# The opening of a retrieval-and-scoring kernel: products nobody reads ahead of the user's part, the second list's products behind chunk 0, chunk 1's load behind slot 6, tile 2's sort behind chunk 0's low part

## What is computed

```
retrieved = jnp.mean(item_embeddings[indices], axis=1)          # indices 512 x 50, table 12500 x 512
fused_rep = jnp.concatenate([user_rep, retrieved], axis=1) @ W_fuse + b_fuse   # 512 x 1024 @ 1024 x 512
logits    = fused_rep @ W_proj + b_proj                          # 512 x 512 @ 512 x 12500, fp32
```

## Time and profile before

| | us |
|---|---|
| median of 3 runs | 310.73 (309.54 to 311.03) |
| the profiled execution | 309.87 |
| its span | 308.0 |
| TensorE busy in it | 296.9 (96%) |
| VectorE busy | 248.3 (81%) |
| ScalarE busy | 128.1 (42%) |
| GpSimd busy | 74.9 (24%) |
| granted TensorE clock, mean | 1.000 |

### The profile page before, as it was taken

One profiled execution on the slowest core, in us unless ns is written; L12 is line 12 of the kernel. 1 busy time (PEld: TensorE's weight loads), 2 busy tenths in 40 slices (PEclk: granted clock), 3 DMA queues, 4 the chain that ended last, 5 costly groups with the idle time before them and its releaser, 6 DMA issues.

```text
span 308.0 us, 4024 instructions
## 1 busy us (share of the span) xinstructions
PE 296.9 (96%) x1384; PEld 242.3 (79%) x1384; DVE 248.3 (81%) x371; ACT 128.1 (42%) x164; POOL 74.9 (24%) x76
## 2 busy tenths in 40 slices
PE   3999999699999999999999999999999999999995
PEld 1559887498888889888887888888888888888884
DVE  5898998778987836999689989979799797996123
ACT  1104664430010012435375575655846458463310
POOL 4766886787777200000000000000000000000000
PEclk9999999999999999999999999999999999999999
DMA  7999999999996322367538966839677494343315
GB/s 271 337 377 312 358 400 377 409 361 403 291 304 211 107 100 69 130 226 277 198 137 324 318 257 220 313 136 292 240 239 295 146 360 159 135 138 128 131 70 199
DMA packets 32547, 75.13 MB, mean 244 GB/s; under 512 B 4511, under 2 KB 20655, under 8 KB 32528
## 3 DMA queue, kind: packets, MB, share of 16 engines
q1 hardware_dynamic: 25264, 58.06, 52.6%
q0 software_dynamic: 5536, 13.73, 13.6%
q10 hardware_dynamic: 1728, 3.10, 2.6%
HBM read 52.85 MB, written 25.60 MB: 255 GB/s over the span
## 4 chain that ended last, share of the span: by engine, by line
PE 80%; DMA 10%; DVE 6%; issue 1%; ACT 1%; POOL 0%; SPq 0%; POOLq 0%; DVEq 0%; ACTq 0%
PE pair L1137 25%; PE pair L1215 15%; PE pair L1217 15%; PE pair L1218 15%; DMA early<-w_proj 7%; PE pair L1083 4%; PE pair L1123 3%; DMA ring<-item_embeddings,rows 2%; DVE w_lo L833 2%; DVE w_lo L919 1%; DMA early<-w_fuse 1%; DVE pair L796 1%; PE pair L1168 0%; DVE t_sums L908 0%; PE pair L1089 0%
## 5 line engine op out<-in xcount | busy, mean ns | idle before, releaser
L440 POOL DMA_INDIRECT ring<-item_embeddings,rows x56 | 59.8, 1067 | 20.3 <-issue 14.0
L1137 PE MATMUL pair<-w_hi,f_hi 128*128 128x500 f32 x144 | 56.7, 394 | 1.8 <-DVE w_lo L833 1.8
L1137 PE MATMUL pair<-w_lo,f_hi 128*128 128x500 f32 x144 | 56.3, 391 | 0.0
L1137 PE MATMUL pair<-w_hi,f_lo 128*128 128x500 f32 x144 | 56.0, 389 | 0.0
L1215 PE MATMUL pair<-w_hi,s_hi 128*128 128x500 f32 x128 | 49.9, 390 | 0.0
L1217 PE MATMUL pair<-w_lo,s_hi 128*128 128x500 f32 x128 | 49.9, 390 | 0.0
L1218 PE MATMUL pair<-w_hi,s_lo 128*128 128x500 f32 x128 | 49.8, 389 | 0.0
L796 DVE SCALAR_TENSOR_TENSOR pair<-ring,mask,pair 128x512 f32<-128x512 f32 x48 | 36.1, 752 | 3.3 <-DVE pair L810 0.5
L1215 PE MATMUL pair<-w_hi,f_hi 128*128 128x500 f32 x96 | 37.3, 389 | 0.1
L1218 PE MATMUL pair<-w_hi,f_lo 128*128 128x500 f32 x96 | 37.2, 388 | 0.0
L1217 PE MATMUL pair<-w_lo,f_hi 128*128 128x500 f32 x96 | 37.2, 387 | 0.0
(11 more groups left out here) (138 smaller groups left out, 433.2 us busy)
## 6 DMA issues: line engine op xcount, KB each, us to landing
w_raw<-w_proj SPq DMA_DIRECT2D x26, 500.0 KB, 8.1
early<-w_proj SPq DMA_DIRECT2D x24, 500.0 KB, 6.7
logits<-part_out SPq DMA_DIRECT2D x21, 500.0 KB, 3.4
logits<-out_sb SPq DMA_DIRECT2D x28, 250.0 KB, 2.3
logits<-out_sb SPq DMA_DIRECT2D x10, 500.0 KB, 3.0
logits<-out_sb ACTq DMA_DIRECT2D x8, 250.0 KB, 7.0
early<-b_proj SPq DMA_DIRECT2D x8, 250.0 KB, 9.9
s_sum<-b_proj SPq DMA_DIRECT2D x8, 250.0 KB, 6.9
```

Source lines behind the costliest of these rows:

```text
L440: return nc.gpsimd.indirect_dma_start(out=to, out_offset=None, in_=table, in_offset=bass.IndirectOffsetOnAxis(ap=column, axis=0), **how)
L1137: m = nc.tensor.matmul(ps[:, 0:CHUNK], f[:, t, k, :], w, start=begin, stop=(f is f_lo and k == HK - 1))
```

## The change

Six edits, all in the first 65 us of the program:

- TensorE starts with 16 products of 256 columns into `total_ps`, which nothing reads; their operand is a piece of the still unused `w_hi`, which VectorE sets to 1.0 as its first instruction (`warm_ready`).
- The products of list 1 (`pack_list(1)`) move from behind the user's part to behind chunk 0 of tile 0. `list_spots(1)` moves behind `split_lo(0)` and has its own scratch in `out_sb`; `list_rows(1)` and `list_taken(1)` move behind `split_lo(2)`. List 1 has a PSUM bank of its own, so that group 2 waits for `list_kept`, the first evacuation waits for both lists, and group 0 and ScalarE's first split wait for list 0 alone.
- `list_rows(0)` and `list_taken(0)` stand behind slot 5's add, not slot 3's. `bias_lo` moves behind `add_last(0)`.
- SyncE loads `wf_ret` ahead of chunk 1, and waits for slot 6 of tile 0 ahead of chunk 1.
- `sort(2)` moves from ahead of `count_columns` to behind `list_spots(1)`. `split_lo(1)` is cut in two around the first f_lo, `split_lo(5)` around `add_home(1)`.
- In chunk 7 of tile 0 `turn_slots` stands directly ahead of `turn_sum(1)`, and both stand ahead of the wait for the second half's low part.

```diff
             sp.dma_start(bf_col[:], b_fuse).then_inc(bf_landed, 16)
+            sp.dma_start(wf_ret[:], wf_dram[1]).then_inc(wf_ret_landed, 16)
+            sp.wait_ge(slot_landed[place(0, 6)], 16 * slot_uses(0, 6))
             load_chunk(1)
-            sp.dma_start(wf_ret[:], wf_dram[1]).then_inc(wf_ret_landed, 16)
...
                 act.wait_ge(projected, c + 1)
+                if c == 0:
+                    act.wait_ge(packed, LISTING)
...
-            act.wait_ge(packed, LISTING)
+            act.wait_ge(packed, 1)
             split_hi(0)
             split_hi(1)
             mean(0)
...
+            nc.vector.memset(warm[:, 0:2 * P].bitcast(F32), 1.0).then_inc(warm_ready, 1)
             number()
...
             sort(1)
-            sort(2)
             count_columns()
             list_spots(0)
-            for i in range(4):
+            for i in range(DVE_FIRST - 1):
                 add(0, i)
             list_rows(0)
             list_taken(0)
-            list_spots(1)
-            for i in range(4, DVE_FIRST):
-                add(0, i)
-            bias_lo()
+            add(0, DVE_FIRST - 1)
             count_left()
             add_last(0)
+            bias_lo()
             dve.wait_ge(laps_ready, 2)
             add_home(0)
             split_lo(0)
-            list_rows(1)
-            split_lo(1)
+            list_spots(1)
+            sort(2)
+            split_lo(1, (0,))
             fused_lo(0, (0,))
+            split_lo(1, (1,))
             add_last(1)
             fused_lo(0, (1,))
             add(1, 0)
             fused_lo(0, (2, 3))
             add(1, 1)
+            split_lo(2)
+            list_rows(1)
             list_taken(1)
-            split_lo(2)
...
-            split_lo(5)
+            split_lo(5, (0,))
             add_home(1)
+            split_lo(5, (1,))
...
             def turn_sum(t):
                 if t == 1:
+                    turn_slots()
...
                 for k in range(HK):
+                    if halfway is not None and k == HK // 2:
+                        turn_sum(halfway)
                     if (begun or c == RESIDENT and t == 0) and k % 2 == 0:
                         pe.wait_ge(lo_ready, 2 * c + k // 2 + 1)
                     if first:
                         pe.wait_ge(f_ready, HK * t + k + 1)
-                    if halfway is not None and k == HK // 2:
-                        turn_sum(halfway)
...
                 if g == 0:
                     pe.wait_ge(bias_lo_ready, 1)
-                    pe.wait_ge(listed, LISTING)
+                    pe.wait_ge(listed, 1)
+                elif g == 1:
+                    pack_list(1)
+                elif g == 2:
+                    pe.wait_ge(list_kept, LISTING)
...
+            pe.wait_ge(warm_ready, 1)
+            for x in range(WARM):
+                nc.tensor.matmul(total_ps[:, 0:2 * P], warm[:, 0:P], warm[:, 0:2 * P], start=True, stop=True)
             user_part(0)
...
             user_part(3).then_inc(user_fused, 1)
-            pack_list(1)
```

21 lines of the change are left out of this document (12 added, 9 removed).

## The result

| | before | after |
|---|---|---|
| median, us | 310.6 (309.54 to 311.46, 12 runs) | 311.43 (310.9 to 312.97, 12 runs) |
| ratio to before | | 1.0033 [1.0019, 1.0047] |
| the profiled execution, us | 309.87 | 311.04 |
| its span, us | 308.0 | 309.2 |
| home add of tile 0 starts, us | 27.63 | 24.92 |

The change made the kernel slower by a third of a per cent: a small loss, but the ratio's interval lies above 1, and the median lies above the predicted range. The granted clock is 1.000 in both. From the start of fuse(1) to the end of the execution it takes 311.04 - 64.81 = 246.2 us, before 309.87 - 63.96 = 245.9 us: of the 1.17 us between the two executions 0.85 are there when fuse(1) starts. The table shows the path: the home add is 2.7 us earlier, and ten microseconds behind it VectorE is late.

What follows compares the result with a forecast made beforehand. The start of fuse(1) was taken to bound the kernel, set by landings, VectorE's queue and TensorE's products. 0.45 us at chunk 6 and 0.1 at chunk 7 put it 0.5 us earlier: median 309.8 us, range 308.2 to 311.1.

Steps and rivals of the forecast that it cites:

- The moment that decides: Start of fuse(1) on TensorE, at 63.96 us before: the whole change is worth its shift; 244 us of products follow.
- Unread products at 0: TensorE's start: 16 products might save 2.0 us in the user's part, but nothing on the path, behind slot 10's landing.
- List 1's products covered: TensorE between chunks 0 and 1: 1.5 us later for the chunks behind, covered by the waiting at chunks 6 and 7.
- Home at 25.6 us: VectorE's home add of tile 0: 2.0 us earlier than 27.63 us, bounds 24.9 and 26.5 us.
- Rival A: Quicker VectorE, home at 24.9 us, and landings moving 1.5 us or more: fuse(1) at 62.0 us, median 308.4 us; chance 0.25.
- The first f_lo at 33.4 us: VectorE behind home: 7.8 us of work from home at 25.6 us, so first f_lo at 33.4 us, against 33.93.
- rival B: Chunk 1's load delays chunk 2's first half, stalling ScalarE and the first f_lo; at 34 us it costs 1.5 us; chance 0.15.
- Rival B's deciding point: Landing of chunk 2's first half at 32.5 us: there the gain is gone; from 32 us every microsecond loses one.
- The loads, "0 to 2 us earlier": SyncE's queue: chunks 2 to 7 land 0 to 2 us earlier, as slot 10 may land 1 to 2 us earlier.
- the sum: Fuse(1) at 59.34 - 0.45 + 4.5 = 63.4 us, taking the landings as early enough for the 0.45 us.
- VectorE's queue, +0.9 us taken up by the gap at chunk 6: VectorE 0.9 us later through chunks 3 to 6; the 1.29 us gap absorbs it, chunk 6's second half starting 0.45 us earlier.
- Chunk 7, worth 0.1 us: TensorE at chunk 7: the turn replaces the wait for the second half, 4.5 us to fuse(1) instead of 4.62.

Runs made afterwards that it cites:

- b_gate: The kernel before without SyncE's wait for slot 10 ahead of chunk 2's load; ratio to before 0.9934.
- b_sort: The kernel before with sort(2) alone moved, to behind list_rows(1) and ahead of split_lo(1); ratio to before 1.0014.
- b_gate_warm: b_gate with the 16 unread products ahead of the user's part; ratio to before 1.0000.
- a_nowarm: The changed kernel without the 16 unread products and the memset of their operand; ratio to before 1.0038.
- a_list: The changed kernel with list 1's steps alone back at their old places, the wait for slot 10 kept; ratio to before 1.0035.
- a_gate_list: a_gate with list 1's steps back at their old places and one PSUM bank for both lists; ratio to before 0.9962.
- a_load: The changed kernel with chunk 1's load back ahead of wf_ret, without the wait for slot 6; ratio to before 1.0042.
- a_fhi: The changed kernel with fused_hi(0) ahead of chunk 2's first half on ScalarE; ratio to before 1.0005.
- a_gate: The changed kernel without SyncE's wait for slot 10 ahead of chunk 2's load; ratio to before 0.9964.
- b_turn: The kernel before with slot 11's turn and turn_sum(1) both between chunk 7's halves, ahead of the wait; ratio to before 1.0013.
- b_mid: The kernel before with turn_sum(1) alone moved ahead of the wait for chunk 7's second low part; ratio to before 0.9956.
- a_sort: The changed kernel with sort(2) back ahead of count_columns; ratio to before 1.0044.
- a_split: The changed kernel with chunk 1's low part whole ahead of the first f_lo; ratio to before 1.0036.
- a_mid: The changed kernel with slot 11's turn back ahead of chunk 7, turn_sum(1) left between its halves; ratio to before 0.9991.

## Why the prediction was wrong

Three steps failed, and at fuse(1) they made 0.85 us later of a forecast 0.5 us earlier. The loads of chunks 2 to 7 were to start up to 2 us earlier; chunk 2 was issued at 27.84 us, before at 27.69. The first f_lo was to come at 33.4 us; ScalarE, behind chunk 2's landing, held it until 34.52. And VectorE was to be 0.9 us late at chunk 6, less than the gap of 1.29 us there; it was 2.0 us late, and the gap's end moved by 0.86 us as well. How the 0.33% of the medians divides among them stays open. By its own steps:

- **The moment that decides** (fuse(1), with a constant 246 us behind it): right, in after and in nearly all the kernels run (245.8 to 246.2 us; b_gate, b_sort and b_gate_warm have 1.2 to 2.3 us more).
- **Unread products at 0**: right in this kernel. a_nowarm shows no difference, and TensorE waits 1.51 us for slot 10 behind them. In b_gate they are not free (b_gate_warm).
- **List 1's products covered**: the medians agree (a_list, a_gate_list), but the cover is thinner than the step said. It put the end of chunk 6 at 57.4 us; chunk 7's first product came at 58.74. The step left chunk 0 where it was, and chunk 0 took 39.48 - 34.83 = 4.65 us, before 3.02, with 1.05 us of waiting for the second f_lo. TensorE was ready for chunk 7's products at 60.20 - 1.07 = 59.1 us, later than the 58.9 us forecast for them. And there is a way by which TensorE's lag comes back that no step of the prediction has: ScalarE's evacuations wait for TensorE, and the high parts of chunks 6 and 7 stand behind them. In after that path would let the high part start at 54.03 us, 0.23 us ahead of the load. In the profiled execution of a_list, where the 1.5 us are taken out, the landings came later still (chunk 6's second high part at 56.00 us, behind a load), so no run isolates that path.
- **Home at 25.6 us**: 24.92, the bound that the step gave. Rival A's other condition, landings that move, wasn't met.
- **The first f_lo at 33.4 us**: this failed in the way of rival B. VectorE was ready at 32.9 us, ScalarE's f_hi came at 34.5. Rival B's deciding point for chunk 2's first half was 32.5 us, and it came at 33.20: by its rule, one for one, 0.7 us; measured 34.52 - 33.93 = 0.59. So place and size at that step are rival B's. Its reason is not: chunk 1's second half had landed by 28.06 us, where ScalarE converts it, 0.2 us behind chunk 2's issue, and a_load, with chunk 1 loaded early, gives nothing back. In 22.0 to 27.84 us SyncE issued nothing, so nothing of chunk 1 stood ahead of chunk 2. Whether every microsecond at this step is one at the end is open: in the profiled execution of a_nowarm the first f_lo is 1.95 us and fuse(1) 1.71 us later than in after, in that of b_sort 3.10 and 0.99 us later than before. In after itself VectorE's queue hands the stall on to chunk 6 (below); for it as a cause of the loss in the medians speaks a_fhi alone.
- **The loads, "0 to 2 us earlier"**: wrong. It reasoned that slot 10 would land 1 to 2 us earlier since GpSimd no longer waits for home. But slot 10's gather stands ahead of home's in GpSimd's order; what GpSimd had waited 1.27 us for the earlier trace rows comes behind it. It left 0.28 us earlier, and the gate opened at 27.84 us. That the chunks behind it are what the time hangs on, a_gate and b_gate show: opened 4.7 us earlier it gives 0.69% (a_gate against after), 2.8 us earlier 0.66% (b_gate against before), the latter with a first f_lo no earlier than before (34.28 us, in an execution 1.5 us above its median). The gain that the sum took for granted needed that edit, and the change doesn't have it.
- **Chunk 2's first half** then took 5.4 us from issue to the start of ScalarE's cast, before 4.9. In one execution that is within the scatter; over the eight kernels of the changed order with gate and f_hi in place it is 4.6 to 6.4 us (mean 5.7), in before, b_turn, b_mid and b_sort 4.4 to 5.8 (mean 5.0). Home of tile 1 leaves at 26.79 us, before at 28.59, and the gathers behind it run beside the load: 30 to 33 us by DMA queue (q1 is SyncE's, q0 the gathers; packets, MB, share of the time), before and after:

```profile
q1 hardware_dynamic: 254, 0.90, 93.9%
q0 software_dynamic: 3, 0.01, 1.7%
```

```profile
q1 hardware_dynamic: 248, 0.89, 76.6%
q0 software_dynamic: 79, 0.26, 24.1%
```

By the Trainium skill, DMA: Bandwidth & Descriptors, "Queues, rings and completion order", each DMA engine goes round-robin between the queues that it has work for. By that rule the gathers would take turns from SyncE's load. In these rows its queue moved 0.89 MB, before 0.90, so they don't bear that out as the reason, and no run isolates another.
- **VectorE's queue, +0.9 us taken up by the gap at chunk 6**: wrong in size, and in taking the gap's end as fixed. VectorE came to chunk 6 2.0 us late, not 0.9; the 1.1 us more are those by which the first f_lo missed 33.4 us. More than 1.29 us the gap could not have taken up, so VectorE alone, ready at 55.15 us, makes 0.7 us of loss in this execution whatever the loads do. The end of the gap moved too: chunk 6's second high part came at 54.26 us, not 53.40. Its last 0.23 us were a load's landing, and right behind it stood ScalarE's own queue, as the rows above show. So three paths end within 0.25 us of each other at chunk 6's second half (VectorE's queue 55.15, ScalarE's about 55.1, the load's 55.32 us), and an edit that took back one of them would have gained little in this execution. It is one execution: in those of a_fhi, a_sort and a_load the high part held VectorE up by 1.5 to 1.6 us there. Part of the reason for that landing is VectorE itself. Chunk 6 goes into chunk 2's raw buffer, and SyncE issues it 1.29 us behind the start of split_lo(2) (37.14 and 38.43 us before, 38.73 and 40.01 after, 36.94 and 38.23 in a_gate), so a lag there is handed to the load; in the chain of after 38.81 and 41.19 are these two links. Only in part: in the six kernels with the gate in place that issue chunk 6 at 38.0 to 38.6 us the high part comes at 53.3 to 56.1 (mean 54.4), in the eight that issue it at 40.0 to 42.0 at 53.8 to 56.0 (mean 55.2), 0.8 us for 2.5. And in four of these fourteen (a_fhi, a_split, a_nowarm, b_sort) the row of that high part names ScalarE's evacuation, not a load, as what ended the wait.
- **Chunk 7, worth 0.1 us**: from the first half's products to fuse(1) it took 64.81 - 60.20 = 4.61 us, before 4.62, forecast 4.5. The length was right, the reading behind it wrong. "The turn takes the place of the wait" looked at the wait between the halves alone; the turn had stood in the wait ahead of chunk 7 (0.79 us) free of charge. The distance between the halves, 2.26 us in the one execution read, made the exchange look even; at 1.5 us it costs 0.7. Over the kernels run the distance is 1.48 to 2.34 us, and I took it for a constant. What the rows show best is another form's worth: with the turn back ahead of chunk 7 and turn_sum left between the halves (a_mid) fuse(1) starts 0.9 us nearer to h0. That the exchange made by the change costs time in the median isn't shown.

What stays open: what a_fhi's edit gives beside the turn's, and so how the 0.33% divides; whether TensorE's lag, through ScalarE's evacuations, has a part in it; and why b_gate_warm loses against b_gate.

## What to carry to other kernels

Before the start of a load is counted as earlier, name the semaphore that it leaves on and follow that back through its own queue: an engine that waits behind that point in its order can be freed without the load moving. Work that can stand in either of two waits belongs in the first of them, and what is left for the second goes there; an exchange that looks even in one execution is priced at the smallest distance that the landings' scatter allows. Idle time that a load ends is slack only if the engine's own earlier work doesn't release that load's buffer, and if nothing else in the queue of the engine between them ends at nearly the same moment: where several paths end within 0.25 us, taking one back gives nearly nothing in that execution. And before a moment of one execution is held against a ratio, look at how far that execution lies from its median.
